# A running sum over graph edges: chunks of 2048 edges instead of steps of 1024

## The reference, cut to what matters

```python
h = jnp.maximum(_layernorm(x), 0.0)
m = jnp.concatenate([h[src], edge_attr_64], axis=1) @ W1a + b1a   # (212500, 128)
m = relu(_bn(m, g1a, be1a))                # mean and variance over all edges
out = segment_sum(m @ W2a + b2a, dst, 12500)
x = x + relu(_bn(concat([h, out]) @ W1b + b1b)) @ W2b + b2b
```

## Time and profile before

| | us |
|---|---|
| three runs: median (lowest to highest) | 6878.51 (6867.25 to 6896.64) |
| profiled execution: span, first to last instruction | 5487.3 |
| median of the runs less that span | 1391.2 |
| stage 4, edge product (L1014 first and last) | 2561.2 to 4641.3 |
| stage 5, running sum (first load to the next stage's first work) | 4666.0 to 5392.3 |
| stage 6, node layer | 5392.3 to 5487.3 |

### The profile page before, as it was taken

The page is one execution under the profiler, slowest core; times in us unless marked ns, Lnnn a source line. Parts: engine busy times, 40 slices in busy tenths (PEclk is TensorE's granted clock), DMA queues, the critical chain, the costliest instruction groups (busy, mean ns, idle before and its releaser), DMA issues. The chain is left out here.

```text
span 5487.3 us, 47739 instructions
## 1 busy us (share of the span) xinstructions
PE 2916.4 (53%) x8675; PEld 1611.3 (29%) x8675; DVE 2048.7 (37%) x2739; ACT 1440.8 (26%) x2694; POOL 3571.2 (65%) x3776
## 2 busy tenths in 40 slices
PE   2035555555555555521555555555555554888887
PEld 2023222332332233210222222222222222455455
DVE  7123333333333333344222222222222223666774
ACT  8011111111111111111222222222222221666663
POOL 6677777777777777766777777777777776111112
PEclk9975555556555655555666666666666666555556
DMA  9623233233233322322333333333333333899992
GB/s 353 207 62 78 78 80 80 77 79 80 78 78 80 80 76 80 80 53 64 105 103 106 107 101 106 107 104 103 107 105 103 107 107 89 311 322 321 321 322 70
DMA packets 396210, 695.12 MB, mean 127 GB/s; under 512 B 138632, under 2 KB 195730, under 8 KB 389410
## 3 DMA queue, kind: packets, MB, share of 16 engines
q1 hardware_dynamic: 250135, 558.29, 29.3%
q0 software_dynamic: 119328, 128.91, 12.4%
q10 hardware_dynamic: 26706, 7.50, 0.6%
HBM read 349.70 MB, written 344.74 MB: 127 GB/s over the span
## 5 line engine op out<-in xcount | busy, mean ns | idle before, releaser
L1014 POOL DMA_INDIRECT pairs<-norm_table,send_idx x1664 | 1573.9, 946 | 526.1 <-issue 506.8
L729 POOL DMA_INDIRECT send_in<-send_table,send_idx x1664 | 1574.3, 946 | 507.7 <-issue 505.1
L1028 PE MATMUL ps_pairs<-ident,pairs 128*128 128x128 f32 x1664 | 400.3, 387 | 991.1 <-issue 744.3
L1131 DVE TENSOR_SCALAR hid<-ps_hid,vec 128x512 f32<-128x512 f32 x416 | 312.2, 751 | 1384.0 <-PE ps_hid L1035 1384.0
L1035 PE MATMUL ps_hid<-pairs_t,w1a 128*128 128x512 f32 x832 | 711.2, 953 | 0.0
L1028 PEld LDWEIGHTS ps_pairs<-ident,pairs 128*128 128x128 f32 x1664 | 262.2, 195 | 1438.9 <-issue 1279.9
L1070 ACT COPY pairs_t<-ps_pairs 128x512 f32<-128x512 f32 x416 | 244.0, 586 | 1473.6 <-PE ps_pairs L1028 1473.6
L741 PE MATMUL ps_msg<-hidden,w_twice 128*128 128x512 f32 x416 | 431.1, 1140 | 307.9 <-ACT hidden L794 307.9
L763 PE MATMUL ps_send<-ident,send_in 128*128 128x128 f32 x832 | 216.3, 410 | 689.7 <-DMA send_in<-send_table,send_idx 689.7
L1254 DVE TENSOR_TENSOR_SCAN total<-ps_mask,total,act_out 128x1024 f32<-128x1024 f32 x208 | 488.8, 2350 | 215.3 <-ACT act_out L1232 215.1
L1201 POOL DMA_INDIRECT node_sums<-hid_edges,end_idx x100 | 94.6, 946 | 643.4 <-SPq L1186 636.9
(11 more groups left out here) (176 smaller groups left out, 3184.6 us busy)
## 6 DMA issues: line engine op xcount, KB each, us to landing
hid_edges<-hid SPq DMA_DIRECT2D x208, 512.0 KB, 2.9
hid<-hid_edges SPq DMA_DIRECT2D x208, 512.0 KB
hid_edges<-rows SPq DMA_DIRECT2D x208, 512.0 KB, 3.8
recv_edges<-node_sums SPq DMA_DIRECT2D x52, 1024.0 KB
recv_in<-recv_edges SPq DMA_DIRECT2D x208, 256.0 KB
max_edges<-max_rows SPq DMA_DIRECT2D x208, 256.0 KB, 2.1
edge_in<-in_edge_attr_dram SPq DMA_DIRECT2D x415, 128.0 KB, 3.1
send_in<-send_table,send_idx POOLq DMA_INDIRECT x1664
```

The lines of the kernel that those rows point to most:

```text
L729: pool.indirect_dma_start(out=send_in[:, s, j, t, :], out_offset=None, in_=send_table, in_offset=bass.IndirectOffsetOnAxis(ap=send_idx[:, ...
L1014: pool.indirect_dma_start(out=pairs[:, s, j, 0:C], out_offset=None, in_=norm_table, in_offset=bass.IndirectOffsetOnAxis(ap=send_idx[:, s / ...
L1028: mm = nc.tensor.transpose(ps_pairs[s % 2][:, j::J], pairs[:, s, j, :], ident[:, :])
L1131: nc.vector.tensor_scalar(part, ps_hid[s % 2][:, :], vec[:, 0:1], None, ALU.add).then_inc(hid_made, 1)
```

## The change

A step of stage 5 becomes a chunk of 2048 edges: one load of 1 MB and one store of 1 MB, both with 8 KB per partition. The compute engines work on a chunk in two halves of 1024 edges, h = 0 and 1. PSUM holds one mask half and one transposed half for each h.

- **DRAM layout.** `hid_edges` is [104, 128, 2048]. Stage 4 stores four blocks at a time (1 MB) from two buffers instead of two blocks from four.
- **Masks.** All of `same_sum` is loaded once, as `masks` [104, 2048]; partition k holds chunk k's mask. The weights of the spreading matmul are column k of a bf16 identity matrix (`row_of`), repeated 128 times, so 104 rows are contracted and row k alone comes through. The 208 small mask loads are gone.
- **Relu in place.** `relu` writes back into `hid` and waits for nothing but the load; `act_out` is gone. A load into one of the 4 `hid` buffers waits for the scan of the chunk that was there, and is issued behind the store.
- **Order.** TensorE: spread(k,0), turn_back(k-1,0), spread(k,1), turn_back(k-1,1). ScalarE: relu(k,0), rows_out(k-2,0), relu(k,1), rows_out(k-2,1), a lag of two chunks. SyncE: store(k-5), load(k), confirm(k-8), in chunks. A transposed piece takes every sixteenth column and needs both scans of its chunk.
- **Loop.** 12 chunks per round, and `pipeline` takes step counts that are no multiple of it: 24 chunks are written out ahead, five rounds loop, 20 chunks are written out behind.

```diff
@@ pipeline
-    for step in range(steps - unroll, steps + last):
+    for step in range((rounds - 1) * unroll, steps + last):
@@ stage 4
-            hid = tensor(s4, "hid", [P, U // 2, 2, BLK])
+            hid = tensor(s4, "hid", [P, U // 4, 4, BLK])
...
-                    if s % 2 == 0:
+                    if s % 4 != 3:
                         return
@@ stage 5, SyncE
                 def load(r, s):
                     k = r * U + s
-                    at_least(sp, relu_done, k - U + 1)
-                    sp.dma_start(hid[:, s, :], hid_v[:, bass.ds(k, 1), :]...).then_inc(loaded[s], 16)
-                    at_least(sp, mask_spread, k - R + 1)
-                    sp.dma_start(mask_in[:, s % R, :], mask_v[:, bass.ds(k, 1), :]...).then_inc(loaded[s], 16)
+                    at_least(sp, sum_done, 2 * (k - HR + 1))
+                    sp.dma_start(hid[:, s % HR, :], hid_v[:, bass.ds(k, 1), :]...).then_inc(loaded[s % HR], 16)
+                    if isinstance(k, int) and k == 0:
+                        sp.dma_start(masks[:, :], same_sum.rearrange("(p c) -> p c", c=CO)).then_inc(masks_in, 16)
...
-                pipeline(sp, STEPS, U, [(0, load), (5, store), (U, confirm)])
+                pipeline(sp, CHUNKS, U, [(5, store), (0, load), (8, confirm)])
@@ TensorE
-                    at_least(pe, loaded[s], 32 * (r + 1))
-                    at_least(pe, sum_done, k - 1)
-                    for a in range(0, STEP, BLK):
-                        mm = nc.tensor.matmul(ps_mask[s % 2][:, a:a + BLK], ones5[:, :], mask_in[:, s % R, a:a + BLK], ...)
+                    if h == 0:
+                        at_least(pe, sum_done, 2 * k - 1)
+                    else:
+                        at_least(pe, sum_done, 2 * k)
+                    one_row = row_of[0:NCO, bass.ds(k, 1)].broadcast_to([NCO, P])
+                    for a in range(0, HALF, BLK):
+                        mm = nc.tensor.matmul(ps_mask[h][:, a:a + BLK], one_row, masks[:, h * HALF + a:h * HALF + a + BLK], ...)
...
+                    if h == 0:
+                        at_least(pe, sum_done, 2 * (k + 1))
+                    at_least(pe, rows_made, 2 * k + h - 1)
+                    for j in range(JS // 2):
+                        mm = nc.tensor.transpose(ps_back[h][:, j * P:(j + 1) * P], total[:, s % 2, h * (JS // 2) + j::JS], ident[:, :])
@@ ScalarE
-                    at_least(act, loaded[s], 32 * (r + 1))
-                    at_least(act, sum_done, k - 1)
-                    nc.scalar.activation(act_out[:, s % 2, :], hid[:, s, :], ACT.Relu, ...)
+                    if h == 0:
+                        at_least(act, loaded[s % HR], 16 * (r * (U // HR) + s // HR + 1))
+                    part = hid[:, s % HR, h * HALF:(h + 1) * HALF]
+                    nc.scalar.activation(part, part, ACT.Relu, ...)
@@ VectorE
+                    at_least(dve, mask_spread, 2 * k + h + 1)
+                    at_least(dve, relu_done, 2 * k + h + 1)
+                    if h == 0:
+                        at_least(dve, back_turned, 2 * (k - 1))
+                    nc.vector.tensor_tensor_scan(total[:, s % 2, part], ps_mask[h][:, :], hid[:, s % HR, part],
+                                                 before, ALU.mult, ALU.add).then_inc(sum_done, 1)
```

More of the change, by code:

```diff
@@ L88, in pipeline @@
     first = 2 if last else 1
-    assert rounds * unroll == steps and rounds > first and last <= unroll
+    assert rounds > first and last <= unroll
     def peeled(step):
@@ L960, in gnn_kernel @@
             gathered = [sem(f"gathered4_{i}") for i in range(U)]
[L961 removed]
+            stored = [sem(f"stored4_{i}") for i in range(U // 4)]
             idx_copied, w_in, turned, copied, multiplied, hid_made, stats_made, root_ready, root_made = (
@@ L1213, in spread, with turn_back @@
                     mm.then_inc(mask_spread, 1)
-                def turn_back(r, s):
+                def turn_back(r, s, h):
                     k = r * U + s
[L1217 to L1220, removed]
+                    if h == 0:
[3 more added lines that the diff above has]
+                        mm = nc.tensor.transpose(ps_back[h][:, j * P:(j + 1) * P], total[:, s % 2, h * (JS // 2) + j::JS], ident[:, :])
@@ L1234, in rows_out, with relu @@
[L1234 to L1240, removed]
+                def relu(r, s, h):
+                    if h == 0:
+                        at_least(act, loaded[s % HR], 16 * (r * (U // HR) + s // HR + 1))
+                    part = hid[:, s % HR, h * HALF:(h + 1) * HALF]
+                    nc.scalar.activation(part, part, ACT.Relu, bias=shift[:, 0:1], scale=gain[:, 0:1]).then_inc(relu_done, 1)
@@ new lines, in rows_out @@
+                def rows_out(r, s, h):
+                    k = r * U + s
+                    at_least(act, back_turned, 2 * k + h + 1)
+                    if h == 0:
+                        at_least(act, stored[s % R], 16 * (r * (U // R) + s // R))
+                    nc.scalar.copy(rows[:, s % R, h * HALF:(h + 1) * HALF], ps_back[h][:, :]).then_inc(rows_made, 1)
+                pipeline(act, CHUNKS, U, [(0, lambda r, s: relu(r, s, 0)), (2, lambda r, s: rows_out(r, s, 0)),
+                                          (0, lambda r, s: relu(r, s, 1)), (2, lambda r, s: rows_out(r, s, 1))])
@@ new lines, in running_sum @@
+                    at_least(dve, relu_done, 2 * k + h + 1)
+                    if h == 0:
+                        at_least(dve, back_turned, 2 * (k - 1))
+                    at_least(dve, sum_done, 2 * k + h)
+                    before = total[:, 1 - s % 2, CHUNK - 1:CHUNK] if h == 0 else total[:, s % 2, HALF - 1:HALF]
+                    part = slice(h * HALF, (h + 1) * HALF)
+                    nc.vector.tensor_tensor_scan(total[:, s % 2, part], ps_mask[h][:, :], hid[:, s % HR, part],
+                                                 before, ALU.mult, ALU.add).then_inc(sum_done, 1)
```

91 lines of the change are left out of this document (43 added, 48 removed).

## The result

The changed kernel takes 6710.51 us (median of 4 runs, 6705.72 to 6711.37) against 6877.78 for the kernel before: a ratio of 0.9752 (95% interval 0.9737 to 0.9767), 167 us less. Forecast were 84 us less and a range down to 6748. The direction was right, the forecast size was half of the measured one.

What follows compares the result with a forecast made beforehand. The prediction took stage 5 to be bound by a circle of waits through ScalarE, with DMA hidden behind it. Stage -90.0, start +2.7 and end +3.2 gave -84.1: 6878.5 to 6794.4 us, range 6748 to 6846.

Steps and rivals of the forecast that it cites:

- the circle: Stage 5 before: transposes, ScalarE's copy, relu and scan wait in turn, 6.65 us per two steps, and bound the stage.
- TensorE's floor of 5.74: Stage 5 after the change: TensorE's transposes and masks back to back take 5.74 us a chunk, the bound among engines.
- rival D: Stage 5: transposes reading every sixteenth column cost double, chunk time 9.68 us, total 7192.7 us, slower; chance 0.04.
- rival B: Stage 5: TensorE's clock rises above 0.50, the DMA's 5.43 us a chunk decides, total 6750.7 us; chance 0.13.
- the forecast's 5.85: Stage 5: predicted chunk time in us, TensorE's 5.74 plus 0.11 disturbance; over 104 chunks 608.4 against 698.4 us.
- The DMA's ceiling of 398 GB/s: Stage 5 transfers: the fastest rate in the rows, from 8 KB stores with indirect DMAs, gives 5.43 us a chunk.
- Disturbance: +0.11 on TensorE's floor: Stage 5: allowance of 0.11 us a chunk for some lateness of transfers; before the change it was 0.07.
- Queues: Stage 5, SyncE: the load issued behind the store still lands in time for the relu, with some 3 us slack.
- Start +2.7 and end +3.2: Edges of stage 5: more bytes ahead of the first mask, +2.7 us; longer last transposes and store, +3.2 us.
- Stage 4 at nothing: Stage 4: GpSimd paces it, so larger stores of four blocks from two buffers cost 0.
- The 1391 us over the span: Whole kernel: the median exceeds the profiled span by 1391.2 us, contents unknown, left unchanged in the forecast.
- Rivals A and C: Stage 5: A, DMA bounds, chunk 6.27 us, total 6838.1, chance 0.27; C, traffic capped at 322 GB/s, 6884.4, chance 0.06.

Runs made afterwards that it cites:

- lag_one: The changed kernel with ScalarE's rows_out copy one chunk behind instead of two: 5454.5 us, ratio 0.9958 to the kernel before.
- after_again: The changed kernel, no edit, run and profiled again on a chip where the kernel before takes 5478 us: 5318.2 us, ratio 0.9708.
- one_row: The changed kernel with each chunk's mask loaded by itself to one partition and one row contracted: 5376.9 us, ratio 0.9818 to the kernel before.
- half_load: The changed kernel loading only the first half of each chunk after the fourth (sums incomplete): 5315.7 us, ratio 0.9703 to the kernel before.
- pairs4: The changed kernel with stage 4's stores of two blocks from four buffers again: 5316.9 us, ratio 0.9706 to the kernel before.

## Why the prediction was wrong, step by step

- **What bounds the kernel before: right.** lag_one puts the circle back into the changed kernel and loses 136 us; after_again's scans no longer wait for the relu.
- **TensorE's floor of 5.74: right for its clock.** At 0.50 one_row has 5.72, and its transposes of every sixteenth column take 426 ns on average, as those of every eighth did (427). That also settles rival D, and with it the slower side: it did not happen.
- **TensorE's work for a chunk, taken at the clock of before (1.90 and 0.97, 5.74 in all): the step that failed.** I costed the new mask matmul by its length and its weight load ("I take the lower end") and left the clock to rival B with a chance of 0.13. Both costs were right: 1.06 us at 1.2 GHz against 1.03 before, and a weight load with a median of 100 ns in both. But with this matmul in place the clock is 0.84, TensorE is busy for 147 of 200 us only, its floor falls below the others, and the forecast's 5.85 has no ground: measured are 5.10 to 5.12, so the stage lost 166 us and not 90. I had seen a row that points there: the earlier trace rows shows 0.91 where 128 rows are contracted, and the earlier trace rows shows 0.50 with one row at 86% busy. The second I used as evidence against B, when it was the very condition that the change removes. I left out the other half of stage 6, where 128 rows are contracted at 0.50 (5440 to 5484, above). So the rows at hand did not decide for B either; the sum needed a term for the clock, and it had none. The rule of the Trainium skill ("TensorE: Matmul & The Clock Gate", Part 1), that sustained activity releases the clock, points to the result; the traces agree only in part, since one_row's TensorE was busy for 200.00 of 200 us and stayed at 0.50.
- **The DMA's ceiling of 398 GB/s: mis-sized.** It was taken from a stretch of stores in stage 1; stage 5 ran at 421 to 423, loads and stores mixed, share 1.01. For rival B I gave a chunk time of 5.43 by it, measured are 5.10. That is 34 us, most of the 40 between B's 6750.7 and the 6710.5 measured, and it is why the range ended too high. The two rows at 345 GB/s and 0.93 that stood at its other end were not limits, since stage 5 went beyond both; half_load has 319 GB/s with a share of 0.91 and loses no time by it. The Trainium skill's 358 GB/s ("DMA: Bandwidth & Descriptors", Specifications) is passed by 64; this kernel runs on one core.
- **Disturbance: +0.11 on TensorE's floor.** Not needed: one_row lies at 5.72, TensorE without a gap.
- **Queues: right in the main.** The load behind the store came in time at 377 GB/s in one_row (one wait, of 7.2 us); at 421 it is late by some 0.9 us at a time (79.8 us in 88 waits), and little of that reaches the scan (4.4 us in after_again).
- **Start +2.7 and end +3.2:** measured +4.3 and +2.5; together 6.8 against 5.9.
- **Stage 4 at nothing: right** (pairs4, and 2075.9 us against 2076.0).
- **The 1391 us over the span:** right to leave as they are. The text ahead of the prediction places them around the span; the profiles place 1313 of them inside stages 3 and 4, on a chip of the other kind.
- **Rivals A and C:** out. A's chunk time of 6.27 was no limit, nor were C's 322 GB/s: stage 5 ran at 5.10 and 422. A was right in this much, that the DMA is now one of the three limits.
- **Rival B: its mechanism came true.** Its time did not, by the DMA's ceiling.

## What to carry to other kernels

A DMA share of 0.93 beside engines that wait for each other need not be a DMA bound: follow one cycle on the timeline, and look whether the consumer of the loads ever waits for them. When two limits lie close, taking one away can show next to nothing (2.4 us here, and 14 with both gone); take both away before you call either harmless. And where a change alters a matmul's rows or weights, read the granted clock at both kinds of matmul in the trace, since every term of TensorE hangs on it.

## What was not expected of the hardware

- TensorE's granted clock stayed at 0.50 with mask matmuls of 1 and of 32 rows, busy for 200.00 of 200 us, and was 0.84 with 104 rows of zeros at 146 of 200. It was 0.50 again in a stretch of stage 6 whose matmuls contract 128 rows.
- Loads and stores mixed ran at 419 to 423 GB/s on one core, and at 417 with 4 KB per partition in place of 8.
- The kernel before took 5478 us on three chips, and 6783 and 6878 in the other two sets of runs; the changed kernel took 5318 and 6711. The changed kernel's two profiles put the difference into the stages that gather through GpSimd, while one gather took 944 to 947 ns (medians) on both.
